# Seven late weight folds moved to an attention block's drain, and two small steps of the drain moved from POOL to DVE

## What is computed

```python
x = x + attn_a(LN(x))     # linear attention, 16 heads, with its own relu FFN
x = x + ffn(LN(x))        # attention over 8 tokens, then a mixture of experts
x = x + attn_b(LN(x))     # attention without softmax, 16 heads of 64
x = x + ffn(LN(x))        # the same weights again
# ffn: y = LN(z + mha(z))*g1+be1;  softmax attention, 4 heads of 32
#      idx = argmax(y @ Wg.T);  h = relu(y @ W1[idx] + b1[idx])
#      out = LN(y + h @ W2[idx] + b2[idx])*g2+be2;  8 experts, F = 512
```

## Time and profile before

| | |
|---|---|
| median of 3 runs | 749.75 us (749.43 to 750.53) |
| profiled execution, its own time | 750.66 us |
| its span | 748.8 us |
| busy share | PE 87%, DVE 70%, POOL 58%, ACT 43% |
| chain that ended last | PE 31%, DVE 29%, POOL 16%, issue 11%, DMA 4% |
| block 0, from its first load to the end of its table | about 176 to 298 us |
| block 1, the same | about 523 to 639 us |

### The profile page before, as it was taken

The page is one execution under the profiler, slowest core; times in us unless marked ns, Lnnn a source line. Parts: engine busy times, 40 slices in busy tenths (PEclk is TensorE's granted clock), DMA queues, the critical chain, the costliest instruction groups (busy, mean ns, idle before and its releaser), DMA issues.

```text
span 748.8 us, 18836 instructions
## 1 busy us (share of the span) xinstructions
PE 652.9 (87%) x5406; PEld 555.9 (74%) x5406; DVE 523.5 (70%) x2049; ACT 321.8 (43%) x829; POOL 438.0 (58%) x951
## 2 busy tenths in 40 slices
PE   5899999987899983899997999997699995699993
PEld 2688888873577873799996787786467875598993
DVE  2578888856999966588884344443799975587884
ACT  2233322311687841455542222221588852355551
POOL 5455555664548885277775443350548887076776
PEclk9999999998999975899999999999799985699997
DMA  7940000004012241232314000000412221222220
GB/s 189 344 161 15 22 14 14 14 22 127 16 36 77 83 163 57 83 82 84 81 56 129 8 23 23 19 16 29 119 31 70 83 85 65 70 83 79 75 73 24
DMA packets 58740, 53.27 MB, mean 71 GB/s; under 512 B 7632, under 2 KB 53628, under 8 KB 58480
## 3 DMA queue, kind: packets, MB, share of 16 engines
q1 hardware_dynamic: 51338, 36.65, 18.0%
q0 software_dynamic: 5568, 12.97, 4.9%
q10 hardware_dynamic: 1766, 2.83, 1.1%
HBM read 31.07 MB, written 19.83 MB: 68 GB/s over the span
## 4 chain that ended last, share of the span: by engine, by line
PE 31%; DVE 29%; POOL 16%; issue 11%; DMA 4%; DVEq 3%; ACT 3%; ACTq 1%; POOLq 1%; SPq 0%
PE wide L1511 4%; POOL sorted_dram L1216 4%; PE bank L1497 4%; PE wide L1484 4%; PE bank L1349 3%; DVE early L753 3%; POOL rstd L1200 3%; DVE hid_f L1401 3%; DVE stats L517 2%; DVEq L1394 2%; POOL rstd L540 2%; DVE z L544 2%; DVE stats L1397 2%; PE wide L462 2%; DVE late L1423 1%
## 5 line engine op out<-in xcount | busy, mean ns | idle before, releaser
L1349 PE MATMUL bank<-zt,late 128*128 128x128 f32 x624 | 93.8, 292 | 3.4 <-DVE hid_f L1401 1.5
L1306 POOL TENSOR_TENSOR rstd<-var_e,half_neg 128x1 f32<-128x1 f32 x78 | 55.4, 710 | 70.2 <-DVE var_e L1411 66.4
L1349 PEld LDWEIGHTS bank<-zt,late 128*128 128x128 f32 x624 | 80.4, 197 | 11.7 <-issue 4.4
L1216 POOL DMA_INDIRECT sorted_dram<-rows_e,pos x64 | 66.2, 1035 | 19.3 <-issue 15.0
L526 POOL TENSOR_TENSOR both_m<-stats 128x2 f32<-128x2 f32 (+1 forms) x54 | 10.8, 200 | 102.4 <-DVE stats L517 102.4
L1382 ACT ACTIVATE late<-we 128x512 f32 x78 | 49.3, 632 | 30.1 <-PE bank L1349 24.1
L1360 PE MATMUL wide<-late,hid_f 128*128 128x128 f32 x416 | 55.2, 276 | 1.2 <-DVE tmp L1407 1.2
L1360 PEld LDWEIGHTS wide<-late,hid_f 128*128 128x128 f32 x416 | 50.6, 192 | 1.7 <-issue 1.2
L1197 POOL TENSOR_TENSOR var_m<-mvs,eps 128x2 f32<-128x2 f32 (+1 forms) x50 | 11.2, 224 | 64.1 <-DVE mvs L1150 30.5
L1401 DVE TENSOR_SCALAR hid_f<-bank 128x256 f32<-128x256 f32 x78 | 33.1, 425 | 21.8 <-PE bank L1349 15.1
L540 POOL TENSOR_TENSOR rstd<-spread_m,half_neg 128x2 f32<-128x2 f32 (+1 forms) x54 | 45.0, 834 | 4.2
(11 more groups left out here) (268 smaller groups left out, 1950.0 us busy)
## 6 DMA issues: line engine op xcount, KB each, us to landing
rows_e<-sorted_dram SPq DMA_DIRECT2D x78, 128.5 KB, 2.2
xa<-x_dram SPq DMA_DIRECT2D x9, 640.0 KB, 6.5
we<-L_ffn_W SPq DMA_DIRECT2D x16, 256.0 KB
x_dram<-xout SPq DMA_DIRECT2D x32, 128.0 KB, 1.8
early<-late SPq DMA_DIRECT2D x128, 32.0 KB
sorted_dram<-L_attn_a_x ACTq DMA_DIRECT2D x2, 1028.0 KB
rows_e<-L_ffn_b SPq DMA_DIRECT2D x1, 2048.0 KB
sorted_dram<-rows_e,pos POOLq DMA_INDIRECT x64, 2.8
```

Source lines behind the costliest of these rows:

```text
L1216: nc.gpsimd.indirect_dma_start(sorted_dram[n][:, :], bass.IndirectOffsetOnAxis(ap=pos[:, p % 3, t:t + 1], axis=0), pay[:, p % PAYS, t, :], ...
L1306: nc.gpsimd.tensor_tensor(rstd[:, s % 3, 0:1], var_e[:, s % 3, :], half_neg[:, 0:1], ALU.pow).then_inc(g["rstd"], 1)
L1349: last = nc.tensor.matmul(to[:, (m % 2) * P:(m % 2 + 1) * P], we_t[:, c1, m * P:(m + 1) * P], zt[:, c1, 0, 0:P], start=True, stop=True)
```

## The change

- The seven later folds leave PE's bodies 1 to 4 of block 0. One each stands now in bodies 17, 18, 19 and 20 (W1 of experts 4 to 7), two in body 21 (second biases), the tiny one in body 22. DVE copies them in its bodies 23 to 27 (one each in 23 to 26, two in 27), behind everything else of the body; ACT copies the tiny one after its last body. They use the banks 1 and 2, which the drain has left.
- The bias rows of experts 4 to 7 no longer come with the first loads. ACT issues a 1024 KB DMA for them into `hid_f` once stage A's last product has been made. DVE waits for it in body 23.
- In both blocks, for pairs 11 to 15, DVE makes variance plus epsilon and minus mean right behind its aggregate (L1092), and POOL only power and shift. DVE waits there on its own aggregate.
- In both blocks, for pairs 12 to 15, DVE adds the payload's middle third in its body p + 11 (bodies 23 to 26), behind the token column, in place of POOL's body p + 8.
- ACT waits ahead of the experts of block 0 until all folds have been kept.

```diff
-        bias_b1 = rows_e
+        bias_b1 = [rows_e[:, 0:E // 2 * F], hid_f[:, 0:E // 2 * F]]
...
+        def bias_rows(half):
+            return f["b1"].rearrange("(h e) n -> h (e n)", h=2)[half:half + 1].to_broadcast([P, E // 2 * F])
...
-                   (bias_b1[:, :], f["b1"].rearrange("(a e) n -> a (e n)", a=1).to_broadcast([P, E * F])),
+                   (bias_b1[0], bias_rows(0)),
...
         def hat_bank(n):
+            if N_A + 10 <= n < N_F:
+                return bank[1 + n % 2]
...
-        HATS_SOON = {1: (10, 12), 2: (12, 14), 3: (14, 16), 4: (16, 17)}
+        HATS_LATE = {PAIRS + 1: (10, 11), PAIRS + 2: (11, 12), PAIRS + 3: (12, 13), PAIRS + 4: (13, 14), PAIRS + 5: (14, 16),
+                     PAIRS + 6: (16, 17)}
...
         @on("scalar")
         def _(act):
+            act.wait_ge(w_o_in, 16 * len(loads_o))
+            act.wait_ge(a_s["w2"], PAIRS)
+            act.dma_start(bias_b1[1], bias_rows(1)).then_inc(w_o_in, 16)
             hat_copies(act, hats_f[:HATS_FIRST], N_A)
...
+        PAY_X_BY_DVE, MEANS_BY_DVE = PAIRS - 4, PAIRS - 5
...
# PE, body i, last step
+                    if n == 0 and i == PAIRS + 1:
+                        pe.wait_ge(g["v"], o + PAIRS)
                     hat_products(pe, *hats_between(n, i))
-                    if n == 0 and i == 5:
-                        pe.wait_ge(hat_kept, N_F)
...
# DVE, aggregate of pair p = i - 11
-                        after(dve, g["step"], ob + p + 7)
+                        after(dve, g["step"], os_ + min(p + 7, MEANS_BY_DVE + 9))
+                        if p >= MEANS_BY_DVE:
+                            after(dve, g["rstd"], ob + p + 7)
+                            after(dve, g["shift"], ob + p + 7)
                         for k in (2, 3):
                             last = nc.vector.bn_aggr(mvs[:, c, k, :], stats[:, c, k, :])
-                        last.then_inc(g["agg1"], 1)
+                        if p < MEANS_BY_DVE:
+                            last.then_inc(g["agg1"], 1)
+                        else:
+                            last.then_inc(g["agg0"], 1)
+                            dve.wait_ge(g["agg0"], oa + PAIRS + p - MEANS_BY_DVE + 1)
+                            nc.vector.tensor_scalar_add(var_m[:, c, 2:], mvs[:, c, 2:, 1], EPS)
+                            nc.vector.tensor_scalar_mul(nmean[:, c, 2:], mvs[:, c, 2:, 0], -1.0).then_inc(g["agg1"], 1)
...
# DVE, token column of pair p = i - 11
+                        if p >= PAY_X_BY_DVE:
+                            nc.vector.tensor_tensor(pay[:, p % PAYS, :, D:2 * D], both(xa, p),
+                                                    b2f[:, :].unsqueeze(1).to_broadcast([P, 2, D]), ALU.add).then_inc(g["pay_x"], 1)
...
+                    if n == 0 and i == PAIRS + 7:
+                        dve.wait_ge(w_o_in, 16 * (len(loads_o) + 1))
                     hat_copies(dve, *hats_between(n, i - 6), of_vector=True)
...
# POOL, body i
+                        if i - 9 < MEANS_BY_DVE:
                         nc.gpsimd.tensor_tensor(var_m[:, c, w], ...)
                         nc.gpsimd.tensor_tensor(nmean[:, c, w], ...).then_inc(g["step"], 1)
...
-                    if has(8):
+                    if has(8) and i - 8 < PAY_X_BY_DVE:
```

More of the change, by code:

```diff
@@ L426, in build @@
                            hat(E, fold_f[:, :], wg_t[:, :], None, wg[:, :], after=N_A + 3)]
-        hats_f += [hat(F, fold_f[:, :], we[:, e, 0:F], None, we[:, e, 0:F], rows=bias_b1[:, e * F:(e + 1) * F])
-                   for e in range(E)]
+        hats_f += [hat(F, fold_f[:, :], we[:, e, 0:F], None, we[:, e, 0:F],
+                       rows=bias_b1[e // 4][:, e % 4 * F:(e % 4 + 1) * F]) for e in range(E)]
         hats_f += [hat(4 * D, fold_f[:, :], ident4, None, we[:, e:e + 4, 2 * F:], rows=bias_b2[:, e * D:(e + 4) * D])
@@ L798, in build @@
         HATS_FIRST = 10
-        HATS_SOON = {1: (10, 12), 2: (12, 14), 3: (14, 16), 4: (16, 17)}
-        assert len(hats_f) == HATS_SOON[4][1]
+        HATS_LATE = {PAIRS + 1: (10, 11), PAIRS + 2: (11, 12), PAIRS + 3: (12, 13), PAIRS + 4: (13, 14), PAIRS + 5: (14, 16),
+                     PAIRS + 6: (16, 17)}
+        assert len(hats_f) == HATS_LATE[PAIRS + 6][1]
         @on("tensor")
@@ L818, in hats_between @@
         def hats_between(n, i):
-            lo, hi = HATS_SOON[i] if n == 0 and isinstance(i, int) and i in HATS_SOON else (0, 0)
+            lo, hi = HATS_LATE[i] if n == 0 and i in HATS_LATE else (0, 0)
             return hats_f[lo:hi], N_A + lo
@@ L847, in attention_block @@
         def attention_block(n, src_dram, stored_before):
-            o, ob = n * PAIRS, n * M_BODIES
+            o, ob, os_, oa = n * PAIRS, n * M_BODIES, n * (MEANS_BY_DVE + 9), n * (2 * PAIRS - MEANS_BY_DVE)
             TT, QV, KB, SB, WO, AV, GB, RB = (bank[k] for k in range(8))
@@ L1041, in _ @@
                 pipeline(act, PAIRS, 8, 1, body, PAIRS)
+                hat_copies(act, *hats_between(n, PAIRS + 6))
             @on("vector")
@@ L1147, in body @@
                         dve.wait_ge(g["stats0"], o + p + 1)
-                        after(dve, g["step"], ob + p - 2)
+                        after(dve, g["step"], os_ + p - 2)
                         for k in (0, 1):
@@ L1191, in body @@
                         if has(0):
-                            pool.wait_ge(g["agg0"], o + i + 1)
+                            pool.wait_ge(g["agg0"], oa + i + 1)
                             after(pool, g["z0"], o + i - 2)
@@ L1196, in body @@
                             after(pool, g["z1"], o + i - 11)
-                        nc.gpsimd.tensor_tensor(var_m[:, c, w], mvs[:, c, w, 1], eps4[:, w], ALU.add)
-                        nc.gpsimd.tensor_tensor(nmean[:, c, w], mvs[:, c, w, 0], minus4[:, w], ALU.mult).then_inc(g["step"], 1)
-                        pool.wait_ge(g["step"], ob + i + 1)
+                        if i - 9 < MEANS_BY_DVE:
+                            nc.gpsimd.tensor_tensor(var_m[:, c, w], mvs[:, c, w, 1], eps4[:, w], ALU.add)
+                            nc.gpsimd.tensor_tensor(nmean[:, c, w], mvs[:, c, w, 0], minus4[:, w], ALU.mult).then_inc(g["step"], 1)
+                            pool.wait_ge(g["step"], os_ + i + 1)
                         nc.gpsimd.tensor_tensor(rstd[:, c, w], var_m[:, c, w], half_neg[:, w], ALU.pow).then_inc(g["rstd"], 1)
@@ L1384, in _ @@
                 act.wait_ge(tabled, n * 2 + 2)
+                if n == 0:
+                    act.wait_ge(hat_kept, N_F)
                 pipeline(act, ET, 2, 3, body, 6)
```

## The result

| | before | changed |
|---|---|---|
| median of 5 runs each, on one chip | 750.01 us (749.43 to 750.53) | 746.83 us (745.75 to 749.18) |
| ratio, 95% interval | | 0.9965 [0.9949, 0.9981] |
| profiled execution, its own time (span) | 750.66 (748.8) | 749.18 (747.1) |
| PE's mean granted clock in it | 0.933 | 0.933 |

A forecast was written before the change was run, and what follows sets the result against it. It took DVE to bind the first softmax bodies and POOL the drains, with PE close at half clock. Terms -3.7 + 0.3 + 0.9 - 3.2 = -5.7 gave 744.0 us on the medians' scale, range 741.0 to 749.2.

The forecast's parts named there:

- The first bodies: Block 0's first four softmax bodies, rid of the folds, shrink to block 1's 15.27 us: -3.7 us.
- Rival E: Block 0's first bodies give nothing, as POOL or PE sets the pace there: 747.7 us, chance 0.05.
- The load: The late 1024 KB load ahead of block 0 may meet the last store of x1: +0.3 us.
- Block 0's rounds: Block 0's drain: POOL relieved, DVE becomes the bound at 4.2 us a round; last power 2.0 us earlier.
- B: PE's clock falls in both blocks' drains as in the kernel before: 748.9 us, chance 0.17.
- D: Folds make PE the bound of block 0's drain at half clock, which loses 6.5 us: 752.9 us, chance 0.08.
- The end of block 0: After block 0's last power, two folds cost 3.4 us (PE 1.9, DVE 1.5), less 0.5 for a better clock.
- Block 1's drain: POOL relieved, rounds of 3.8 us instead of 4.6 with PE's clock mostly up: -3.2 us.
- rival C: PE's clock falls in one drain only: 747.2 us if block 0's, 745.8 if block 1's; chance 0.19.
- The low end of that term: Block 1's drain if PE's clock falls as before: only the last two powers gain, some 1.5 us in all.
- C's other case: PE's clock falls in block 0's drain only: 747.2 us; both cases together have chance 0.19.
- rival F: In both drains DVE's payload add holds POOL, eight adds of 0.42 us: 747.4 us, chance 0.06.

The follow-up runs named there:

- e1: Changed kernel with POOL given back its variance, mean and payload-add steps, so only the folds and their load moved: 750.53 us, ratio 1.0004.
- e5: Kernel before with only the bias-row load split and its second half issued late by ACT: 749.87 us, ratio 0.9996.
- e4: Changed kernel plus one unused PE product in block 1's body 17, ahead of the payload's turn: 744.61 us, ratio 0.9938.
- e9: Changed kernel run again, unaltered: 747.04 us, ratio 0.9971 against the kernel before.
- e12: Changed kernel, two second-bias folds back in body 1, unused products in block 1's body 17 (one) and both blocks' body 21 (two), a repeat: 742.20 us, ratio 0.9916.
- e8: Kernel before plus one unused PE product in block 1's body 17: 747.92 us, ratio 0.9993.
- e3: Changed kernel with the two second-bias folds put back into block 0's body 1: 747.76 us, ratio 0.9972.
- e2: Kernel before with only POOL's steps moved to DVE in both drains, folds and load as before: 748.44 us, ratio 0.9980.
- e10: Changed kernel with two second-bias folds back in block 0's body 1 and one unused product in block 1's body 17: 742.22 us, ratio 0.9931.

## Why the prediction was partly wrong

**The first bodies** (-3.7): right. S fell by 4.03 us in the profiled execution and by 3.45 in e1, whose clock was 0.96 there; the length of block 1's bodies was the right measure of what is late next. Rival E is out.

**The load** (+0.3): the pieces agree. From DVE's last result row of stage A (`xout`, 172.63; before 173.76) to the second statistics of block 0 (180.68; 181.58) went 8.05 us, against 7.82. As a whole it is too small for a timed run (e5).

**Block 0's rounds** (-2.0): right in size, but not for the reason given. From pair 10's power to pair 15's it took 20.87 us, against 23.23: -2.4. I had made DVE the bound, busy for 4.2 us a round; it was busy for 13.68 us in the four, 3.4 each. What holds the two middle rounds is the row of ACT, PE with its fold (1.05 us) and DVE with its copy (0.60); without the folds and at the same clock the rounds are 3.94 us (e4's R1, 15.74). That 4.2 was met (4.1) is in part luck. Rivals B and D need a low clock in these rounds, and it did not come in any of the nine executions with folds there.

**The end of block 0** (+3.4 - 0.5): mis-sized. The folds stood on the last chain as foretold, but it grew by 4.7 us where 2.9 were booked. The stretch still ran at 0.50 for the most part (0.55 in the mean), so that two folds cost PE 3.4 us and not 1.9, and the half microsecond that I had booked for a better clock was not there. In e9 the clock was up for part of it (T0 11.34), in e4 up to 283.4 (9.91, with 1.72 us in the chain for the same four instructions). Against e12's 6.47, which has no folds there and the clock at 1.00 all through, e4's 9.91 is 3.4 more: the price of the folds themselves was right, and the clock was what it lacked. Together with the rounds, block 0's drain is +2.4 instead of +0.9.

**Block 1's drain** (-3.2): this is the step that failed, by its last sentence, "I take the upper side because the pause ahead of L950 shortens". It did shorten, to 1.17 us where I had said 1.2. But the clock fell behind it, PE held the last two rounds (5.35 and 5.15 us, where 3.8 were reckoned), and the term was worth 0.4 us. One row of a 1.22 us pause with the clock up could not carry the conclusion that pauses of this length are harmless; e9 shows pauses of 1.15 and 1.29 us with a different outcome each. Where the clock was held up, the term came out as reckoned: in e4 from pair 10's power to pair 15's 20.19 us, against 23.28 before, -3.1. A clock that falls in block 1 alone is one case of rival C, priced at 745.8 us, 1.0 below the median; C's other case, 747.2, is nearer by number, but the clock did not fall so.

**The low end of that term** (-1.5) was too kind as well. I had pair 15 follow "one round of 3.5 to 3.8 us behind". PE's last body at the low clock lasted 5.15 us, as estimated (5.2), but PE held both of the last rounds. Before, the clock was back for the last body of PE, at 620.9; now it was still down. The stretch from there to the last statistics, before and then changed:

```profile
620.90:624.20 3.30, 2.99 (x23) 2.58 (x24) 2.50 (x14) 1.91 (x5) 2.87 (x6) 1.00 0.11 40
```

```profile
620.90:624.00 3.10, 3.10 (x17) 3.10 (x16) 2.12 (x15) 0.77 (x2) 2.00 (x3) 0.50 0.21 77
```

So what the relief had given in the first two rounds, 1.2 us, was taken back in the last two.

**DVE's add holding POOL** (rival F): out at its price, though not in kind. By instructions of single lines (duration ns min/median/max):

```profile
L1182 DVE TENSOR_TENSOR rows_e<-xa,b2f x8: 420/421/452, 266.2 to 625.1; 128x256 f32<-128x256 f32 x8
...
L1227 POOL TENSOR_TENSOR rstd<-var_m,half_neg x50: 692/721/1042, 180.2 to 623.9; 128x2 f32<-128x2 f32 x36, 128x4 f32<-128x4 f32 x14
```

The add is 0.42 us, and POOL's power keeps its 0.72. Only one of the eight met a power (at 277.47, within the power of 276.87), and both kept their lengths. In block 1 one add met POOL's shift, which began 0.02 us after it:

```profile
610.35 0.42 DVE L1182 TENSOR_TENSOR rows_e<-xa,b2f 128x256 f32<-128x256 f32 x1
610.37 0.45 POOL L1229 TENSOR_TENSOR shift<-nmean,rstd 128x2 f32<-128x2 f32 x1
```

The shift takes 0.20 us elsewhere; here it ended 0.05 us after the add. In the kernel before it was the other way round. DVE's L1144 of 0.60 us began at 622.32 within POOL's add (622.16 to 622.89) and ended just behind it. So the sharing of interfaces that the Trainium skill describes ("GPSIMD Engine Reference", section 1, Specifications) shows in the traces in both directions. In these meetings the instruction that began second ended just behind the first. For POOL that was 0.25 us once in block 1 and 0.07 in block 0, not eight times 0.42. The stretch on DVE's side is gone with POOL's add (its line is now L1165, 0.17 to 0.21 us in block 1's drain).

**The sum** by what was measured: -4.0 + 0.2 + 2.4 - 0.4 = -1.8, and the profiled execution was 1.5 us faster than that of before (its span 1.7). That these agree is in part luck. Stage A was 1.1 us shorter up to its last `xout`, and from the table of block 0 to the first row maximum of block 1 it took 244.42 us in place of 243.30, 1.1 longer. Neither is in the forecast, and e8 shows that stage A differs by as much between executions of one program. At the medians it is 3.2. By e9 (R1 15.79) some executions also get the 2.7 us of block 1. How many of the timed ones do can't be read from their times. The mean clocks hint at few, though they mix all stages: e9's profiled run has 0.944, three more of the changed kernel's 17 runs have 0.942 to 0.944, and the other thirteen at most 0.938. This stays open. Open too is what makes the clock fall in one execution and not in the next at the same place.

## What to carry to other kernels

When two engines are close to being the bound, relief of the one is worth nothing for certain until the other's worst case is below it too: here 2.7 us lay behind PE's clock, and one unused product in PE's pause released them. The same product without the relief gave nothing, and the relief without the product gave nothing in that block's four rounds in four profiled executions of five. Work moved "to where there is room" has to be fitted round by round: one fold a round cost 0.1 to 0.2 us, a second 1.4 to 1.6, and behind the last pair each fold counted in full and mostly at half clock. A single row in which a pause left the clock up is no price; give such a term both ends and a chance, or put the filler in, which held the clock in four executions of four here.

## What was not expected of the hardware

- The same pause in the same program ends either way. A fall came after 1.17 us (changed, block 1), 1.18 (e3, L963 at 602.38), 1.29 (e9, its second), 1.39 (e2, block 0) and 1.58; the clock stayed through 1.15 (e9), 1.29 (e4, its second) and 1.37 (changed, block 0). What PE has to do around the pause counts. In block 0's drain the clock kept up through 1.37 to 1.68 us in all nine executions with the folds there and fell in all four without them; in block 1's it held in all four with the filler. Why it also held once without either (e9) stays open.
- More PE work made the kernel faster: e4 has one product more than the changed kernel, and 5.1 us less PE busy time in its four rounds.
- The kernel before itself spreads from 746.7 to 752.6 us over 33 runs on one chip, so that a version's single profiled execution can differ by as much as the whole effect. Part of such differences arises ahead of the blocks. Block 0's first row maximum is at 190.36 us in the kernel before and at 187.17 in e8, the same program up to there. In the five executions with a clock of 1.00 in the first 50 us (e3, e4, e8, e10, e12) it is at 187.0 to 188.1, in the other eight (0.90 to 0.97) at 188.9 to 191.6. The lengths S, R and T repeat to 0.1 us where the clock ran the same course (R0 16.40 to 16.44 in seven executions).
